# Flamingo stack: the routing of chunk 6 spread over six steps of the last attention chunk

## The reference

```python
# fourth attention: 16 heads of 64, softmax over the context, one projection
scores = jnp.einsum('bqhd,bkhd->bhqk', q * SCALE, k)
attn = jax.nn.softmax(scores, axis=-1)
out = jnp.einsum('bhqk,bkhd->bqhd', attn, v).reshape(B, SQ, INNER)
x = x + jnp.tanh(g_xattn[3]) * ((out @ w_out + b_out) * jnp.tanh(gate[0]))
...
# fourth feed-forward: each token (layer-normed) goes to 4 of 16 experts
dist2 = jnp.sum((x[:, :, None, :] - keys) ** 2, axis=-1)
topv, topi = jax.lax.top_k(-dist2 + x @ rw.T + rb, TOP_K)
w = jax.nn.softmax(topv, axis=-1)
```

## Time and profile before

| | us |
|---|---|
| median of 3 runs (lowest, highest) | 1583.37 (1582.58, 1584.12) |
| profiled execution, its own time | 1582.47 |
| its span on the core | 1580.7 |
| TensorE busy | 1380.3 (87%) |
| VectorE busy | 1102.3 (70%) |
| ScalarE busy | 1015.8 (64%) |
| GpSimd busy | 538.1 (34%) |

### The profile page before, as it was taken

The page is one execution under the profiler, slowest core; times in us unless marked ns, Lnnn a source line. Parts: engine busy times, 40 slices in busy tenths (PEclk is TensorE's granted clock), DMA queues, the critical chain, the costliest instruction groups (busy, mean ns, idle before and its releaser), DMA issues.

```text
span 1580.7 us, 34386 instructions
## 1 busy us (share of the span) xinstructions
PE 1380.3 (87%) x9974; PEld 1029.7 (65%) x9974; DVE 1102.3 (70%) x3531; ACT 1015.8 (64%) x2931; POOL 538.1 (34%) x640
## 2 busy tenths in 40 slices
PE   4788887988899988998999999999976299999994
PEld 3566665676744465443666666666666199999994
DVE  4788877687777667883666876776665466666665
ACT  2688887554555564225788777777764377777762
POOL 3363468222211411010003242242144445555550
PEclk9999999999999999999999999999987599999998
DMA  8100059500499910000000010010034122222227
GB/s 195 25 8 7 14 83 175 84 0 14 92 175 180 146 34 21 1 0 7 1 8 25 12 34 24 12 35 17 21 126 161 40 62 64 66 66 64 63 57 266
DMA packets 143412, 98.24 MB, mean 62 GB/s; under 512 B 20598, under 2 KB 132515, under 8 KB 142155
## 3 DMA queue, kind: packets, MB, share of 16 engines
q1 hardware_dynamic: 134602, 80.09, 25.6%
q0 software_dynamic: 8704, 16.87, 3.2%
HBM read 43.03 MB, written 54.93 MB: 62 GB/s over the span
## 4 chain that ended last, share of the span: by engine, by line
PE 61%; ACT 13%; DVE 11%; issue 10%; another core or an unknown queue 2%; DMA 1%; SPq 1%; POOL 0%; DVEq 0%; ACTq 0%; POOLq 0%
PE bank L1442 7%; PE bank L1450 7%; PE bank L1008 6%; PE bank L1294 4%; PE bank L1024 4%; ACT arena L1483 4%; PE bank L949 3%; ACT att L1620 3%; PE bank L1059 3%; PE bank L1012 2%; ACT att L1485 2%; PE bank L1044 2%; PE bank L1034 2%; PE bank L1370 2%
## 5 line engine op out<-in xcount | busy, mean ns | idle before, releaser
L1483 ACT ACTIVATE arena<-bank 128x512 f32<-128x512 f32 (+7 forms) x380 | 245.7, 675 | 151.4 <-PE bank L1357 54.0
L1900 ACT ACTIVATE att<-bank,arena 128x128 f32<-128x128 f32 x576 | 165.1, 372 | 71.2 <-PE bank L1442 69.9
L822 POOL DMA_INDIRECT expert_outputs<-arena x144 | 146.2, 1016 | 146.0 <-issue 105.1
L1620 ACT ACTIVATE att<-bank,arena 128x128 f32<-128x128 f32 x512 | 180.7, 395 | 17.8 <-DVE arena L2158 16.7
L776 POOL DMA_INDIRECT dispatched_rows<-arena x112 | 113.0, 1009 | 177.2 <-DVE arena L2047 116.2
L1450 PE MATMUL bank<-arena,att 128*128 128x128 f32 x1152 | 153.8, 277 | 2.7 <-ACT att L1900 1.5
L609 POOL TENSOR_TENSOR ve<-mv,eps 128x4 f32<-128x4 f32 x64 | 13.0, 202 | 417.6 <-DVE mv L1963 408.1
L1442 PE MATMUL bank<-xnT,arena 128*128 128x128 f32 x1152 | 154.1, 277 | 0.2 <-ACT xnT L1483 0.2
L1450 PEld LDWEIGHTS bank<-arena,att 128*128 128x128 f32 x1152 | 140.6, 192 | 5.2 <-ACT att L1900 5.2
L1442 PEld LDWEIGHTS bank<-xnT,arena 128*128 128x128 f32 x1152 | 141.6, 194 | 0.8 <-ACT xnT L1483 0.8
L2625 DVE COPY arena<-arena 128x512 f32 x144 | 61.9, 430 | 84.7 <-issue 84.2
(11 more groups left out here) (381 smaller groups left out, 3244.6 us busy)
## 6 DMA issues: line engine op xcount, KB each, us to landing
dispatched_rows<-padf SPq DMA_DIRECT2D x16, 2128.5 KB, 31.7
arena<-dispatched_rows SPq DMA_DIRECT2D x144, 64.5 KB
cxT<-in_ctx SPq DMA_DIRECT2D x32, 256.0 KB
arena<-in_L_ffn_w SPq DMA_DIRECT2D x8, 1024.0 KB
arena<-expert_outputs SPq DMA_DIRECT2D x8, 1024.0 KB, 14.2
expert_outputs<-arena POOLq DMA_INDIRECT x144
out_x<-x SPq DMA_DIRECT2D x8, 256.0 KB, 4.3
dispatched_rows<-arena POOLq DMA_INDIRECT x112
```

What stands on the lines that cost most here:

```text
L822: pl.indirect_dma_start(sent_out, bass.IndirectOffsetOnAxis(xtu3[:, s, P:P + 1], 0), yt3[:, s, :], None, bounds_check=TOP3 * TOKENS - 1, o ...
L1483: copy = lambda o, i: nc.scalar.activation(o, i, ACT.Copy)
L1620: last = nc.scalar.activation(ex3_of(w, side)[:, i, :], bank[side][:, i * P:i * P + P], ACT.Exp, bias=nm3[:, w % 2, h:h + 1], accum_out=su ...
L1900: last = nc.scalar.activation(h3[:, s % 2, k * P:k * P + P], bank[s % 2][:, k * P:k * P + P], ACT.Gelu, bias=b1c3[:, s % 4, k:k + 1])
```

## The change

The last chunk gets its own order. On VectorE the units 6, 7, 8, 9, 10 and the first half of 12 (named 13) are put on the steps 2, 3, 4, 5, 6 and 7, one for each, where two steps carried two units before; unit 6 goes behind the step's `normal`, and the second half of 12 (named 14, the expert weights) goes into the drain. `residual_half(c, 0)` and unit 6 of the first half of chunk 7 go behind the `values` and `normal` of step 7. On TensorE the units 8, 9 and 12 go behind the `probs_T` of their step, and 12 from step 5 to step 6. On ScalarE unit 8 goes from step 3 to step 4, unit 9 from step 5 to behind the `probs_T` copies of step 4, unit 10 from step 5 to step 6. In the drain unit 8 goes behind `probs_T` on both. No instruction is added or taken away on any engine; GpSimd's and SP's programs are the same.

```diff
 # TensorE, body
-                        if live and not more and w in (3, 4, 5):
-                            routing(c - 1, {3: 8, 4: 9, 5: 12}[w])
-                        if not live:
-                            routing(c - 1, {0: 8, 1: 9, 2: 12}[w], 0)
+                        if not live and w:
+                            routing(c - 1, {1: 9, 2: 12}[w], 0)
                         if (live and w >= 1) or (not first and w < 1):
                             probs_T(c, w - 1)
+                        if live and not more and w in (3, 4, 6):
+                            routing(c - 1, {3: 8, 4: 9, 6: 12}[w])
+                        if not live and w == 0:
+                            routing(c - 1, 8, 0)
...
 # ScalarE, body
-                        if live and not more:
-                            for u in {3: (8,), 5: (9, 10)}.get(w, ()):
-                                routing(c - 1, u)
-                        if not live:
-                            for u in {0: (8,), 1: (9,), 2: (10,)}[w]:
-                                routing(c - 1, u, 0)
+                        if live and not more and w == 4:
+                            routing(c - 1, 8)
+                        if not live and w:
+                            routing(c - 1, {1: 9, 2: 10}[w], 0)
                         for side in range(2):
                             if (live and w >= 1) or (not first and w < 1):
                                 probs_T(c, w - 1, side)
...
+                        if live and not more:
+                            for u in {4: (9,), 6: (10,)}.get(w, ()):
+                                routing(c - 1, u)
+                        if not live and w == 0:
+                            routing(c - 1, 8, 0)
...
 # VectorE
-                        if live and not more:
-                            for u in {2: (6,), 3: (7, 8), 5: (9, 10), 6: (12,)}.get(w, ()):
-                                routing(c - 1, u)
-                            if w == 7:
-                                residual_half(c, 0)
-                                routing(c, 6, 0)
...
+                def last_body(c):
+                    for w in range(PAIRS):
+                        maxima(c, w)
+                        if w == 2:
+                            residual(c - 1)
+                        if w in (3, 4, 5, 6, 7):
+                            routing(c - 1, {3: 7, 4: 8, 5: 9, 6: 10, 7: 13}[w])
+                        values(c, w - 2)
+                        for side in range(2):
+                            normal(c, w, side)
+                        if w == 2:
+                            routing(c - 1, 6)
+                    residual_half(c, 0)
+                    routing(c, 6, 0)
+
+                def drain(c):
+                    routing(c - 2, 14)
+                    values(c, -2)
+                    routing(c - 1, 7, 0)
+                    routing(c - 1, 8, 0)
+                    values(c, -1)
```

More of the change, by code:

```diff
@@ L2037, in routing @@
                     v.tensor_reduce(ohs3[:, of, :], oh3[:, qs, :].rearrange("p (j k) e -> p j e k", j=n), AX, ALU.add).then_inc(sem("F3_chosen"), 1)
-                if u == 12:
+                if u in (12, 13):
                     dve.wait_ge(sem("F3_routing"), c * 3 + 3)
@@ L2047, in routing @@
                     v.tensor_copy(places[:, qs], to3[:, qs]).then_inc(sem("F3_rows_ready"), 1)
+                if u in (12, 14):
                     dve.wait_ge(sem("F3_exp"), c + 1)
@@ L2200, in residual_half @@
                         step(last)
[L2202 to L2206, removed]
-                            residual(c - 1)
-                        if live and not more:
-                            for u in {2: (6,), 3: (7, 8), 5: (9, 10), 6: (12,)}.get(w, ()):
-                                routing(c - 1, u)
-                            if w == 7:
-                                residual_half(c, 0)
-                                routing(c, 6, 0)
[L2214 to L2224, removed]
@@ new lines, in drain, with body @@
+                def drain(c):
[4 more added lines that the diff above has]
+                    values(c, -1)
+                    routing(c - 1, 9, 0)
+                    routing(c - 1, 10, 0)
+                    residual_half(c - 1, 1)
+                    routing(c, 6, 1)
+                    routing(c - 1, 12, 0)
+                def body(c, first=False, ahead=True):
+                    for w in range(PAIRS):
+                        maxima(c, w)
+                        if w == 2 and not first:
+                            residual(c - 1)
+                        if not first:
@@ L2225, in body @@
                             for u in {2: (6,), 3: (7,), 4: (8,), 5: (9,), 6: (10,), 7: (12,)}.get(w, ()):
                                 routing(c - 1, u)
-                        if (live and w >= 2) or (not first and w < 2):
+                        if w >= 2 or not first:
                             values(c, w - 2)
-                        if live:
-                            normal(c, w, 0)
-                        if more and ahead and 3 <= w < 7:
+                        normal(c, w, 0)
@@ L2232, in body @@
+                        if ahead and 3 <= w < 7:
                             front(c + 2, w - 3)
-                        if live:
-                            normal(c, w, 1)
+                        normal(c, w, 1)
                 def rest():
@@ L2241, in rest @@
                         front(1, k)
-                    body(0, 0, True, True)
+                    body(0, first=True)
                     for c in range(1, NC - 2):
[L2244 to L2247, removed]
+                        body(c)
+                    body(NC - 2, ahead=False)
+                    last_body(NC - 1)
+                    drain(NC)
                 return front, rest
```

## The result

Beside each other on one chip the kernel before took 1583.32 us (median of 8 runs, 1580.41 to 1584.17) and the changed kernel 1588.01 (8 runs, 1585.49 to 1589.37): ratio 1.0029, 95% interval 1.0020 to 1.0038, so 4.7 slower. The predicted 1585.1 with its range up to 1588.7 holds the time, but "within 0.2%", my likeliest class, does not. The profiled execution has a span of 1585.8 and a time of its own of 1587.97 (before 1580.7 and 1582.47).

What follows compares the result with a forecast made beforehand. The last sixteen sends were taken as the bound, with GpSimd's and VectorE's clocks running toward them. Late rows put GpSimd at 1232.8 against 1231.14, +1.7, VectorE's side below that: 1583.37 + 1.7 = 1585.1, range 1582.2 to 1588.7.

Steps and rivals of the forecast that it cites:

- What bounds the kernel: Last sixteen sends start the expert layer; GpSimd's and VectorE's clocks run toward them, VectorE's now later by 4.24.
- Step 2: Chunk 7's attention: variance comes 2.2 later, covered by the maxima of the next step; cost 0.
- Step 3: Chunk 7's attention: next scores wait only for the exponentials, a gain of 1.55; their maxima at 1179.0.
- Step 4: Chunk 7's attention: TensorE's `project` waits for ScalarE's copy, idle from 1179.0 to 1183.2; next maxima 4.6 late.
- M: Time of VectorE's maxima of step 5 in chunk 7: predicted 1191.3 against 1186.72 before.
- rival 2: TensorE stays at half clock through step 4, giving M 1195.2 and +5.6; chance 0.20, 0.25 with a late VectorE side.
- the upper end: TensorE's queue from `project` to M all at half clock: 3.8 + 8.2, M at 1195.2.
- Steps 5 to 7: End of chunk 7's attention: 4.4 come back in step 5; R = M + 14.9 = 1206.2, 5.9 later.
- R: Time when the rows of chunk 6 are ready for GpSimd's sends: 1200.3 before, predicted 1206.2, free up to 1204.5.
- GpSimd's length: From R to the end of the first of the last sixteen sends: 26.6, giving 1232.8 against 1231.14, +1.7.
- VectorE's side: The drain: `residual_half` some 4 later still reaches the stall of 5.70 near its end; cost 0 to +1.5.
- The 3.22: GpSimd's gap before its 114th send, during the last sixteen sends: stays, as GpSimd's program is unchanged.

Runs made afterwards that it cites:

- copy_step3: Changed kernel with only ScalarE's unit 8 of chunk 6 put back to step 3, behind the `probs_T` copies: 1561.01 against 1561.87 of the kernel before, ratio 0.9991.
- hold_alone: Kernel before with only ScalarE's unit 8 of chunk 6 moved from step 3 to step 4: 1586.24 against 1580.18 of the kernel before, ratio 1.0036.
- b2_late: Changed kernel, with SP loading the second bias only once VectorE has chosen the first half's experts: 1566.4, one run.
- after_again: The changed kernel, nothing altered, run again on the chip of hold_alone: 1584.3, ratio 1.0023 to the kernel before.
- seven_ahead: copy_step3 plus VectorE's unit 10 in step 5, 13 in 6, TensorE's 12 in 5, GpSimd's first-half deviation behind seven sends, not four: 1557.98, ratio 0.9980 to before.
- copy_step3_2: Second run of copy_step3, on another chip: ratio 0.9999 to the kernel before.

## Why the prediction was right, and where its sum was off

- *What bounds the kernel*: right. The changed kernel's sends decide when the expert layer starts, and an A that is shorter moves the time only if B keeps its length.
- *Step 2, at 0*: right, VectorE's unit 7 waits 0.27 for GpSimd's deviation.
- *Step 3, maxima of step 4 at 1179.0*: 1178.77. The reason given isn't quite the one: the scores did wait for more than the exponentials, namely for unit 8's transposes, ahead of which TensorE stood 3.09 until 1175.61, and started behind them at 1176.66.
- *Step 4, the term that decides*: right in kind and size. The copy ended at 1182.89 (predicted 1183.2), `project` took 3.39 (3.4), M was 1190.34 (1191.3). Copy_step3 takes the stop out and hold_alone puts it in, and the time follows both. In this execution the clock recovered behind `project`, so rival 2's M of 1195.2 did not come. That differs by execution: from the start of `project` to M it is 7.3 here, 8.4 in hold_alone and 8.9 in b2_late, where 0.50 was granted until 1190 and 1174, 4.4 and 5.0 behind that start. None has the 12.0 of the upper end. The reading of the Trainium skill's rule (TensorE: Matmul & The Clock Gate, Part 1) that keeps the whole queue at the half level is not what the rows of 1186 to 1188 show.
- *Steps 5 to 7, R = M + 14.9*: 14.3, R = 1204.6 instead of 1206.2 (the maxima of step 7 came at M + 10.4, not M + 11.0).
- *GpSimd's length, R + 26.6*: too long. Where GpSimd never stands (after_again, copy_step3, seven_ahead and three more) B is 24.0 to 24.5, and with 1.03 for the send that is R + 25.0 to 25.5; the send behind the power took 1.03 in the changed kernel, not 1.5. On GpSimd's side alone R = 1204.6 would have cost nothing.
- *VectorE's side at 0 to +1.5*: this step failed. It was +3.8 in the profiled execution, and it is the whole loss up to the sends. I had read the 5.70 of the earlier trace rows as a stall beside the load of the second weights, which stays where it is while the rest slips against it. Holds of 5.2 to 5.4 stand in the earlier chunks without that load, and on the chip of copy_step3 the load runs at up to 442 GB/s without a hold: the load is neither needed for one nor enough. In the changed kernel that stall shrinks to 1.28 (VectorE's second `values` starts at 1216.69), and a longer one of 8.76 stands one wait later, ahead of `residual_half`. `residual_half` starts 25.4 behind the cast of the rows in before and 25.0 in the changed kernel: it moved with R. The trace of before alone couldn't show that. But the 5.70 was a wait whose end no row named, and such a wait deserved a price of up to R's own delay, and the late VectorE side more than the 0.05 it had beside rival 2.
- *The range held by its width*: the term that gave the +1.7, GpSimd's side, was worth nothing, and the one left at 0 to +1.5 gave the 3.8. That 1588.01 lies under 1588.7 isn't owed to the sum.
- *The 3.22 stays*: right, 3.18 in the changed kernel and 3.12 to 3.30 in the twelve other traces.

That after_again shows the slack as predicted, and its own time of 1580.02 lies 4.3 below the median of its runs, fits with most executions having the long hold. I argue that from one trace; it isn't shown. On the chips of the 1562 kind the kernel before was never traced, so how much slack it has there stays open. What holds TensorE's completions back on the others is open too.

## What to carry to other kernels

When an operation is moved behind another on one engine, look for the queue on a second engine that has its consumer in front of unrelated work: one copy of 0.6, moved one step down, stopped TensorE for 4.25 and cost 6.1 by itself, while the rest of the reordering won nothing measurable. When the profile shows slack, ask what ends the wait on the other side and whether that moves with the term you make late; GpSimd's 4.2 of idleness took up 0.4 of rows that came 4.3 later, nothing of 6.6, and 5.4 of 6.0 in the one execution in which the hold was short. And when a producer comes earlier, look at each wait of the consumer in turn: the time won on the rows showed only after the variance step had been moved as well.

## What the runs showed of the hardware

- TensorE's work may be done by its rows and its waiter go on up to 10 later: `project` had its row until 1219.49, its waiter started at 1229.50. Such waits were there in the six traces of the chips with 1583 and 1580, chunk after chunk, on VectorE and ScalarE alike and ending within 0.06 of each other, and, between 850 and 1260, in none of the eight of three other chips; the kernel took some 20 less there.
- GpSimd has a gap of 3.12 to 3.30 ahead of its 114th send in every trace, whatever stands around it, and in twelve of the fourteen one of 3.53 or 3.54 ahead of the 128th indirect DMA behind that; in the other two a wait for VectorE stands there (4.09 and 3.36).
- TensorE's clock was granted at about half behind 4.25 of idleness and at 1.00 from 1186 on, in the same queue of work; in b2_late, behind 4.24, it was 0.50 for 5.0 of that queue. `project` took 2.02 to 3.75 at this place, and the same kernel had 3.28 in copy_step3 (clock 0.69 and 0.50 in the stretches it lies in) and 2.02 in copy_step3_2 (clock 1.00).
